# Layer 0's cross-attention on fp32 row groups, the two batches staggered behind it, and another order on SyncE's queue

## What is computed

```python
x_norm = modulate(_ln(x), shift_a, scale_a)
qkv = x_norm @ W_qkv + b_qkv
...
attn_w = jax.nn.softmax(jnp.einsum('bhqd,bhkd->bhqk', q, k) * scale, axis=-1)
attn_out = jnp.einsum('bhqk,bhkd->bhqd', attn_w, v)
...
x = x + gate_a[:, None] * attn_out
q_c = _ln(x) @ W_qc + b_qc
kv_c = _ln(context) @ W_kvc + b_kvc
...
c_attn_w = jax.nn.softmax(jnp.einsum('bhqd,bhsd->bhqs', q_c, k_c) * scale, axis=-1)
c_attn_out = jnp.einsum('bhqs,bhsd->bhqd', c_attn_w, v_c)
```

## Time and profile before

| | |
|---|---|
| median of 3 runs | 469.78 us (467.94 to 474.18) |
| the profiled execution | 472.4 us, of which the span from first to last instruction is 470.6 us |
| mean granted clock of TensorE | 0.833 |
| TensorE / VectorE / ScalarE / GpSimd busy | 79% / 64% / 43% / 23% of the span |

### The profile page before, as it was taken

How to read it: one execution, slowest core, us unless ns; L and a number is a source line. 1 busy time by engine, 2 the same in 40 slices (tenths; PEclk the granted TensorE clock), 3 DMA queues, 4 the chain that set the end, 5 groups by cost and what they waited for, 6 DMA issues and landing times.

```text
span 470.6 us, 8977 instructions
## 1 busy us (share of the span) xinstructions
PE 372.1 (79%) x3326; PEld 219.7 (47%) x3326; DVE 303.3 (64%) x1279; ACT 204.3 (43%) x304; POOL 109.5 (23%) x128
## 2 busy tenths in 40 slices
PE   0958839999989988899888788988584566675886
PEld 0735212332333156677655457764362344454454
DVE  4377928999988056666327352234979999996332
ACT  1141016666756935566432133322452555554411
POOL 8047235000010021001014100011434544444010
PEclk9979658999999998999989595556657777776989
DMA  7237560000000000000000000000000000000000
GB/s 212 50 109 219 171 168 1 2 2 3 2 1 2 0 1 1 1 2 3 0 1 1 6 1 7 3 3 0 2 2 1 1 2 1 1 1 1 1 23 24
DMA packets 10811, 12.16 MB, mean 26 GB/s; under 512 B 2378, under 2 KB 9103, under 8 KB 10767
## 3 DMA queue, kind: packets, MB, share of 16 engines
q1 hardware_dynamic: 10469, 11.55, 8.7%
q0 software_dynamic: 256, 0.01, 0.0%
q10 hardware_dynamic: 42, 0.01, 0.0%
HBM read 8.69 MB, written 2.62 MB: 24 GB/s over the span
## 4 chain that ended last, share of the span: by engine, by line
PE 53%; DVE 28%; ACT 7%; issue 7%; DMA 3%; POOL 1%; SPq 1%; ACTq 0%; DVEq 0%
PE psum L1328 6%; PE psum L1388 5%; PE psum L1356 5%; PE psum L1341 5%; DVE mx L1103 4%; DVE left L1158 4%; DVE left L1165 3%; PE psum L1229 3%; PE psum L1487 3%; PE psum L1371 3%; DVE top L1155 3%; PE psum L1399 2%; DVE top L1162 2%; PE psum L1455 2%; PE psum L1411 2%
## 5 line engine op out<-in xcount | busy, mean ns | idle before, releaser
L1103 DVE TENSOR_REDUCE mx<-psum 128x1 f32<-128x512 f32 x128 | 80.1, 681 | 15.1 <-PE psum L1328 15.0
L717 ACT ACTIVATE big<-psum 128x1024 f32<-128x1024 f32 x64 | 62.3, 1022 | 46.0 <-PE psum L1341 45.7
L547 POOL TENSOR_TENSOR rstd<-vareps,minus_half 128x4 f32<-128x4 f32 x12 | 12.2, 1019 | 199.4 <-DVE vareps L887 199.3
L1328 PE MATMUL psum<-KS,QS 72*128 72x512 bf16 x128 | 49.2, 417 | 5.2 <-DVE mx L1103 4.0
L1388 PE MATMUL psum<-kblk,qf 128*128 128x308 f32 x128 | 48.0, 508 | 1.1 <-DVE qf L1036 0.8
L1399 PE MATMUL psum<-ident,pr 128*77 128x128 f32 x256 | 39.6, 306 | 8.9 <-POOL pr L658 8.8
L1341 PE MATMUL psum<-QS,KS 75*128 75x512 bf16 x128 | 39.4, 395 | 7.8 <-issue 7.3
L1399 PEld LDWEIGHTS psum<-ident,pr 128*77 128x77 f32 x256 | 35.7, 172 | 17.2 <-POOL pr L658 12.0
L658 POOL TENSOR_TENSOR pr<-pr,early 128x616 f32<-128x616 f32 x16 | 23.9, 1493 | 56.7 <-ACT early L827 39.5
L1356 PE MATMUL psum<-big,V 128*9 128x512 f32 x256 | 34.3, 608 | 0.5 <-ACT big L717 0.5
L1328 PEld LDWEIGHTS psum<-KS,QS 72*128 72x128 bf16 x128 | 11.7, 102 | 45.7 <-DVE mx L1103 23.7
(11 more groups left out here) (191 smaller groups left out, 677.8 us busy)
## 6 DMA issues: line engine op xcount, KB each, us to landing
QS<-scr_q SPq DMA_DIRECT2D x8, 288.0 KB
KS<-scr_k SPq DMA_DIRECT2D x8, 288.0 KB
scr_q<-qp SPq DMA_DIRECT2D x2, 384.0 KB, 5.6
scr_k<-kp SPq DMA_DIRECT2D x2, 384.0 KB, 6.2
early<-in_L_xcond_w_ada_dram SPq DMA_DIRECT2D x1, 576.0 KB, 8.6
wmlp<-in_L_xcond_W_mlp_dram SPq DMA_DIRECT2D x2, 256.0 KB, 3.4
scr_k<-kp SPq DMA_DIRECT2D x2, 256.0 KB, 6.5
wm<-in_L_xcond_w_m_dram SPq DMA_DIRECT2D x1, 512.0 KB, 7.1
```

What stands on the lines that cost most here:

```text
L717: freed(act.activation(pT[:, u % 2, 1024 * half:1024 * (half + 1)], ps, ACT.Exp), "sT", 0, u, half)
L1103: freed(dve.tensor_reduce(mx[:, n % 3, NT * hh + q:NT * hh + q + 1], ps, AX_X, ALU.max), "max", t, q)
L1328: filled(pe.matmul(ps, QS[b][0:ROWS, h, q * P:(q + 1) * P], KS[b][0:ROWS, h, :], start=True, stop=True), "max", j, q)
```

## The change

**Cross-attention of layer 0.** The same scheme as in layer 1's windows, now for 77 context tokens. The query and key weights are spread with blanks to 32 columns per head (`spread_cross`, GpSimd), so that q (`qcF`) and k (`kcF`) come out of the projection in four row groups of 32; there are 4 such projections (c = 0 to 3) of 128 x 512 per batch in place of 1. For each 128 queries, `cross_maxima` makes 16 products (stationary 8 rows x 128 queries, moving 8 rows x 77 keys; four heads of the same row group one after the other fill one bank) and VectorE reduces each bank of 4 heads. The maxima are turned once per batch, negated and sent by SyncE into the ninth row. `cross_sT` then makes 4 products of 77 x 512 per c, one per row group; ScalarE exponentiates 77 x 1024 twice per c; `cross_out` multiplies by V with the ones' column, four heads on four column groups. VectorE turns the result by a 32x32 transpose of 128 x 512, divides, and after the fourth c transposes once more to have channels in the partitions. The rows of `W_cproj` are loaded in the order that this leaves (4 DMAs for 1). The max-subtraction, the turns on TensorE and ScalarE's copies of layer 0's cross-attention are gone.

**Order.** Batch 0's cross queries and maxima are put into the last steps of the self-attention (t = 32 to 38). Behind it a list, `STAGES`, gives the order: batch 0's S^T and V, batch 1's queries and maxima, batch 0's MLP, batch 1's S^T and V, batch 0's window projections and maxima, batch 1's MLP amid batch 0's windows, and so on.

**SyncE's queue.** Batch 0's stack first, then group 0's rows of maxima, then batch 1's scratch write and its groups one at a time between the rows of maxima; layer 1's other weights behind group 4's.

```diff
+STAGES = """
+    S00 S01 o1 V00 p1 S02 V01 S03 V02 l1 V03 q10 q11 P0 q12 q13 m10 m11 L0 m12 m13 t1 h00 h01 h02 h03 S10 M0 S11 V10 S12 V11
+    S13 N0 V12 a00 a01 V13 a02 a03 v0 P1 x00 x01 x02 x03 y0 L1 h10 h11 h12 h13 E0 E1 M1 F0 E2 F1 G0 E3 F2 G1 N1 F3 G2 a10 a11
+    G3 a12 a13 v1 x10 x11 x12 x13 y1 oT out E4 E5 F4 E6 lnT F5 G4 E7 qc G5
+    """.split()
...
-            for b in range(B):
-                stack_traffic(sp, b)
+            scratch_out(sp, 0)
+            for g in range(NG):
+                stack_in(sp, 0, g)
             for n, (b, g) in enumerate(groups):
                 max_rows(sp, b, G * g, G, n, n % 2, s_mrow[n % 2], 3 * (n + 1))
                 if n == 0:
+                    scratch_out(sp, 1)
+                if n < NG:
+                    stack_in(sp, 1, n)
+                if n == NG:
                     for name, key in (("wso", "w_so"), ("wqc1", "w_q"), ("wco", "w_co"), ("wm1", "w_m1"),
                                       ("wm2", "w_m2")):
                         load_w(sp, name, "L1_xcond_" + key)
+            for b in range(B):
+                cross_max_rows(sp, b)
...
+            def cross_out(b, c):
+
+                u = NQ * b + c
+                ps = read_room(dve, "pvx", b, c)
+                freed(dve.transpose(turned[:, u % 2, :], ps), "pvx", b, c)
+                wait_read(dve, "pvx", b, c)
+                tv = turned[:, u % 2, :].rearrange("p (k e) -> p k e", e=QUAD)
+                r = rdenx[:, u % 2, :]
+                dve.reciprocal(r, tv[:, :, D]).then_inc(s_rdenx, 1)
...
+            def cross_maxima(b, i):
...
+                for j in range(NQ):
+                    ps = open_room(pe, "cmax", b, i, j)
+                    rows = slice(QUAD * j, QUAD * j + D)
+                    for c in range(NQ):
+                        last = pe.matmul(ps[:, c * S:(c + 1) * S], qcF[rows, b, c, i * P:(i + 1) * P], kcF[rows, c, b, :],
+                                         start=True, stop=True)
+                    filled(last, "cmax", b, i, j)
...
+            def cross_sT(b, c):
+                if c == 0:
+                    pe.wait_ge(s_crow[b], 16 * NQ)
+                for half in range(2):
+                    ps = open_room(pe, "sTc", b, c, half)
+                    for t in range(2):
+                        rows = slice(QUAD * (2 * half + t), QUAD * (2 * half + t) + DV)
+                        last = pe.matmul(ps[0:S, t * N:(t + 1) * N], kcF[rows, c, b, :], qcF[rows, b, c, :],
+                                         start=True, stop=True)
+                    filled(last, "sTc", b, c, half)
```

More of the change, by code:

```diff
@@ L104, in rooms_in_turns @@
     use("M", "mods", 0)
-    for layer in range(2):
-        for b in range(B):
[L107 to L115, removed]
-        else:
[L117 to L203, removed]
@@ L204, in rooms_in_turns @@
+    use("M", "oT", 3, 1)
+    use("M", "out", 4, 1)
+    use("M", "out", 5, 0)
+    use("M", "lnT", 5, 1)
+    for c in range(NC_):
+        use("X", "mlp", 1, 1, c)
+        use("W", "mlpb", 1, c)
+    use("M", "out", 5, 1)
     return turn
@@ new lines, in _ @@
+            for part in range(2):
+                ps = read_room(act, "kcF", part)
+                for c in (2 * part, 2 * part + 1):
+                    r, at = VECS["L0_b_kvc"], B * S * (c % 2)
+                    ins_ = act.activation(kcF[:, c, :, :], ps[:, at:at + B * S].rearrange("p (b s) -> p b s", b=B),
+                                          ACT.Identity, bias=colsF[:, c, r:r + 1])
+                freed(ins_, "kcF", part)
+            ps = read_room(act, "kc", 1)
+            c = VECS["L1_b_kv"]
@@ L1203, in _ @@
+            for c in range(NC_):
+                gate_mul(0, c)
+            residual(4, 1)
+            ln_stats(5, 1)
+            ln_norm(5, 1)
+            residual(5, 0)
+            for c in range(NC_):
+                gate_mul(1, c)
+            residual(5, 1)
         @block.tensor
@@ new lines, in cross_out @@
+            def cross_out(b, c):
+                u = NQ * b + c
+                if u == 0:
+                    wait_read(pe, "vc", 0)
+                ps = open_room(pe, "pvx", b, c)
+                for half in range(2):
+                    wait_read(pe, "sTc", b, c, half)
+                for j in range(NQ):
+                    last = pe.matmul(ps[QUAD * j:QUAD * j + DV, :], vc[:, 0, b, NQ * c + j, :],
+                                     pT[0:S, u % 2, j * N:(j + 1) * N], start=True, stop=True)
+                filled(last, "pvx", b, c)
@@ new lines, in _ @@
+            for b in range(B):
+                ln_T(0, b)
+            for b in range(B):
+                qk(b)
+            wide_rows(2)
+            for b in range(B):
+                v(0, b)
+            ps = open_room(pe, "ctxT")
+            pe.wait_ge(s_chat, B)
+            for l2, src in enumerate((chat, ctxt)):
+                for b in range(B):
+                    last = pe.transpose(ps[:, (l2 * B + b) * S:(l2 * B + b + 1) * S], src[:, b, :], ident[0:S, 0:S])
+            filled(last, "ctxT")
@@ L1602 @@
+            o_turn(3, 1, "pvcT", B * NT - 1)
+            project(4, 3, 1)
+            mlp_out(5, 0)
+            ln_T(5, 1)
+            for c in range(NC_):
+                mlp_in(1, 1, c)
+            mlp_out(5, 1)
 _INS = ["x", "cond_1024", "ctx_1024",
```

1140 lines of the change are left out of this document (660 added, 480 removed).

## The result

The changed kernel took **499.99 us** (median of 4 runs, 499.07 to 506.1), against 470.5 (4 runs, 467.94 to 474.18) for the kernel before on the same chip: ratio 1.065, 95% interval 1.054 to 1.076, slower. The forecast was 501. Its profiled execution has a span of 498.1 us and a mean clock of 0.78 (before: 470.6 and 0.833). In experiments 1, 3 and 8 the profiled execution is the slowest of its four (469.3, 507.9 and 512.0 us, where the others go down to 460.1, 500.3 and 504.3); the ratios leave out executions that are over 1.5% slower than the fastest of their kernel.

What follows compares the result with a forecast made beforehand. TensorE was taken to bound the rewritten part, by its work and its clock. From a span of 470.6 us, -7.3 + 1.3 + 5 - 9 gave 460.6, and +41 for the clock 502, stated as 501 (range 485 to 518).

Steps and rivals of the forecast that it cites:

- SyncE's queue: Before the first S^T: the new DMA order removes TensorE's stall from 58.74 to 66.07 us, -7.3 us.
- the same and the keys before the loop: Before the loop: the queue's -7.3 us, and +1.3 for layer 0's keys taking 4 products for 1.
- TensorE's work at full clock: Layer 0's cross-attention: 46.3 us of TensorE's work go out and 51.5 come in, taken as +5 us.
- staggering, with the wait for rows: Behind the loop: other batch's work fills 12 of 15 us idle, batch 1's window maxima rows cost +3; -9 us.
- clock: From the loop's last steps on: the small maxima products pull TensorE's clock to half, +41 us, bounds 0 and 60.
- layer 1's cross-attention and tail: The last stretch of the kernel should keep its 150.6 us.
- the bound of 2 that I gave: Before the loop: upper bound in us for the delay by layer 0's extra key products, taken as 1.3.
- The maxima's product: Layer 0's cross-attention: each of 128 small products costs 0.23 us at full clock, between 0.13 and 0.36.
- The signs that I named: Trace marks, including first S^T near 59 us and maxima of 128 queries in 3.4 to 3.8, about 7 at 0.50.
- The clock did not hold: Rival: TensorE's clock holds, 460 us, or falls only in batch 1's maxima, 473; chance 0.22.
- The cheap product (0.13): Rival: maxima products cost 0.13 us each; 447 with the clock held, chance 0.13; 478 with it fallen, chance 0.07.
- S^T products overlap: Layer 0's cross-attention: four cost 0.86 us together; rival without overlap, or with load and product in succession, 518 to 540, chance 0.08.

Runs made afterwards that it cites:

- experiment 1: The kernel before with only the changed kernel's order on SyncE's queue: 465.0 us, ratio 0.976.
- experiment 3: The changed kernel with the cross maxima's products of two banks alternating between two row groups: 503.5 us, ratio 1.059.
- experiment 8: The changed kernel without staggering, the list behind the loop in the order of the kernel before: 510.8 us, ratio 1.079.
- experiment 5: The kernel before without the maxima and their subtraction in layer 0's cross-attention: 465.9 us, ratio 0.994.
- experiment 6: The kernel before without the maxima of layer 0's cross-attention and with SyncE's new order: 458.0 us, ratio 0.971.
- experiment 4: The changed kernel without the maxima of layer 0's cross-attention (products, reductions, turns and DMAs left out): 458.9 us, ratio 0.965.
- experiment 9: The whole changed kernel, maxima kept, with layer 0's cross-attention S^T on 32 rows per group: 492.7 us, ratio 1.044.
- experiment 10: The changed kernel with cross-attention S^T on 32 rows per group and the cross maxima's products on 128 rows: 495.0 us, ratio 1.046.
- experiment 2: The changed kernel with the cross maxima's products on all 128 rows in place of 8: 503.5 us, ratio 1.061.
- experiment 7: The changed kernel without layer 0's cross maxima and with its S^T on 32 rows per group: 451.1 us, ratio 0.957.

## Why the prediction was right, and where not

The time and the main cause were right, but the time came out closer than its terms. By its own steps, in us of the span:

| step | forecast | measured |
|---|---|---|
| SyncE's queue | -7.3 | -7.0 to -7.7 by itself (5 and 6) |
| the same and the keys before the loop | -6.0 | -4.4 at the first S^T, -3.3 at the loop's end part |
| TensorE's work at full clock | +5 | about -2.5, with a product of 0.17 in place of 0.23 |
| staggering, with the wait for rows | -9 | +6.6 of idle time |
| clock | +41 | about +28, what is left of the 25.8 of busy time |
| layer 1's cross-attention and tail | 0 | -1.6 |
| sum (the first row is part of the second) | +31 | +27.5 |

The sum uses the -3.3 of the second row. The split between work and clock is an estimate: TensorE's busy time from the loop's end to layer 1's cross-attention, each stretch times its granted clock, is 18.48 x 1.00 + 133.88 x 0.81 = 126.9 before and 20.34 x 0.99 + 20.54 x 0.52 + 137.30 x 0.68 = 124.2 after, 2.7 less, which fits the -2.5.

**Luck.** The staggering was off by some 16 us one way, the clock by 13 and the work by 8 the other way, and they nearly cancel. That 501 stands next to 500 is in part luck; what the prediction had right is that the maxima's clock decides, and where.

**SyncE's queue and the keys.** The queue was right, and the stall is gone. In experiment 6, with the kernel before's keys, the first S^T starts at 58.52, where I said near 59 (in experiment 1 at 60.59); in the change at 61.68. There the keys' products take 2.42 us, and VectorE's first row maximum starts 2.15 later (41.98, before 39.83). That is above the bound of 2 that I gave. The earlier trace rows shows 0.53 for one such product, not 0.26; but the same four take 1.31 at full clock in experiments 4, 9 and 10, 0.78 more than one, which is 3 x 0.26. What was missed is the clock: it was 0.50 from 37 to 40 us in this execution, and 1.00 there in the kernel before. The remaining 1 us is the clock further on (0.59 from 45.0 to 58.5 us, 0.70 in experiment 6). It differs from run to run: experiments 4, 9 and 10, with the same list up to there, start S^T at 59.05, 60.77 and 60.37.

```profile
36.95 2.42 PE L1674 MATMUL psum<-ctxT,kblk 128*128 128x154 f32 x8 [0.52 <-ACT ctxT L825]
41.98 4.86 DVE L1195 TENSOR_REDUCE mx<-psum 128x1 f32<-128x512 f32 x8
```

**The maxima's product.** I took 0.23 from a product of 128 loaded columns on all rows; on 8 rows it is 0.17, and 0.30 rather than 0.46 at half clock. On 128 rows (experiment 2) it is 0.24, the row's value. So the nearest row was the nearest in columns but not in rows. The term was too large by 128 x 0.06 = 7.7 at full clock, which carries the work from +5 to about -2.5. The signs that I named missed by it too: a block of 128 queries took 2.79 and 4.81, where I had 3.4 to 3.8 and about 7. With the clock's term it shows in the loop's end: +21.5, where 14.8 for four blocks and 18.5 for the clock had given 33.

**Staggering: the step that failed.** Two errors lay in it. I counted 12 of the 15 us of idle time of the kernel before as what the new order would recover, since I took it for chains through the norms. But waits for normed tokens were 2.6 us of it; other scores already stood between, and the rest lay in waits of 3.8 us and less inside the cross-attention and the windows. The new cross-attention has 8 pieces where there were 16, and its own list without staggering exposes 35.5 us of idle time (176.07 less 140.55) where before had 20.2. Staggering gives 7.8 of that back and about 3 through the clock (experiment 8), so it is worth about the 9 that I gave it, but from a worse start. The wait for the rows of batch 1's window maxima, priced at 3, is 1.6; one that I did not price, for the rows of batch 0's cross maxima, is there too: 2.89 before 188.88, since only a product with V and one turn stand between the turn of the maxima and S^T.

**The clock.** Right in kind and in place: 0.99 up to 164, 0.52 from there, after two blocks where I had one and a half steps, and down in batch 1's maxima. Its size was over-counted with the products: a block of 16 costs 2.0 more at half clock (4.81 less 2.79), where I had 3.7. What brings it down was shown by taking rows away and adding them: with the maxima on 128 rows the loop's end stays at 1.00 (experiment 2); with S^T on 32 rows in place of 9, 0.58 becomes 0.88 with the same instructions (experiment 7). The rule of the Trainium skill ("TensorE: Matmul & The Clock Gate", Part 1) that I set against it, a gate that watches how busy TensorE is, does not fit these rows, if busy is what the profile calls so: busy 20.54 of 20.60 us, at 0.52.

**The rivals.** The clock did not hold. The cheap product (0.13) is met a little over half-way, at 0.17, the point that I gave as deciding for a held clock; with a fallen one it decides nothing. S^T products overlap: four in 1.10 at full clock, 0.24 more than the 0.86 of the sum, 1.9 us for 8 groups. TensorE waited for VectorE's reductions of the cross maxima only once behind the loop, 0.7 us before the turn of the maxima.

**What stays open.** The 41 to 47 us of the maxima are split into work, clock and waits by subtraction, not by a run each: no run holds the clock and keeps the 8-row products. Why the clock falls with 128 rows in a pure stretch of small products, and in the windows with 32, the runs don't say.

**A version that beats both.** With maxima, the kernel before with the new queue (465, ratio 0.976). Without them, the change with S^T on 32 rows (451), some 20 us below the kernel before. It gives up the protection against large scores, which the inputs here don't need; whoever needs it keeps the first.

## What to carry to other kernels

Price a small product by its columns and its rows, and at both clocks; then ask what the clock does to the dense work beside it; here what came with the products cost about as much as the products themselves. If a contraction uses 8 of 32 rows of a group, contract over zeros up to 32 where the data are there anyway: S^T took 1.10 us either way at full clock, and the kernel gained about 7 us. And the idle time of an old schedule does not say what a new order will recover; count the waits of the new list without the new order first.

## What the runs showed of the hardware that I had not expected

- An fp32 product with a load of 128 columns and 77 moving ones takes 0.17 us on 8 rows and 0.24 on 128, in a row of such products at full clock.
- Contraction rows that hold only zeros raised the granted clock: 0.58 to 0.88 over some 20 us with the same instructions (experiments 4 and 7).
- A stretch of 64 such products falls to half clock even on 128 rows (0.53 in experiment 2), and 32 rows change next to nothing in the windows (3.67 for 3.68).
- Alternating two row groups brings a 128-column product from 0.17 to 0.14, not to the 0.03 of the products with 64 columns.
